# Attention scores moved to the end of TensorE's slot, and masks ahead of the attention's addition on VectorE

## The chip, the cores and the metric

One core of one Trainium2 chip. The metric is the device time of one execution, in microseconds (us), as the median over several runs. Engines are named as in the profile: PE is TensorE (PEld its weight loads), DVE is VectorE, ACT is ScalarE, POOL is GpSimd, SP the engine that issues all DMAs here. A name with q (SPq) is the engine's queue.

## What is computed

x has 8 sequences of 1024 rows with 256 columns. The output is x plus two branches of its layer norm xn: a linear attention with Taylor features (the first part of the kernel, which the change doesn't touch), and a transformer of two layers (the second part). One layer, cut to what matters:

```python
h = shift_token(x)                      # second half of the columns comes from the row before
q, k, v = split(h @ wqkv)               # 8 heads of 64
q, k = rotary_xpos(l2norm(q) * qs, l2norm(k) * ks)
o = softmax(mask(8 * q @ k.T)) @ v      # a row sees itself and the 128 rows before
x = x + o @ wo
h = shift_token(x)
h = (h - mean(h)) / sqrt(var(h) + 1e-5) * lg + lb
a, g = split(h @ w1 + b1)
x = x + (a * gelu(g)) @ w2 + b2
```

## The kernel before

`transformer_block` works on tiles of 128 rows. There are four threads: two streams (four sequences each, one behind another) by two layers. A step is one tile of one thread, 4 x 32 = 128 steps in all; they are numbered n and handed out in turn, so that layer 1 of a stream follows its layer 0. Each step passes through four stages, and all engines run a list of slots in which four neighbouring steps are each at another stage: `cur` (projections, norm and rotation of q and k, their transposes), `att` (scores, softmax, attention, out-projection), `nrm` (residual addition, layer norm), `ffn` (up, GELU, down); `nxt` only has its input transposed. Every engine has its own `slot` function, written out by hand, and takes its instructions strictly in that order; semaphores join the engines, and a wait is on a count that the step's number gives.

PSUM has eight banks, given out by name at L692 to L694. What the change and the steps of the prediction touch:

- TensorE, `slot` from L1446: `scores` of att (L1352 and L1359, 64x64 tiles, first in the slot), `project` K and Q (L1327), `up` (L1431, L1436), `project` V, `prob_T` (L1370, L1374), `down` (L1443), `attend` (L1389 middle, tiles of 128x64; L1399 corners, 64x64), `heads_T` K and Q of cur (L1332), `x_T` of nxt (L1319, L1320), `hn_T` of nrm (L1415), `out_project` of att (L1408). A float32 matmul counts as two instructions, a transpose as one.
- `heads_T` of K waits for `k_unit`, the K normalisation on VectorE (L1069); `scores` waits for `kT_ready` and `qT_ready`, ScalarE's copies (L1235, L1240).
- VectorE, `slot` from L1157: the attention's addition `add_attention` (L1108), `mask_scores` four times (L1079 adds the mask and takes the maximum, L1086), `row_statistics` (L1113 on x1, L1115 on the shifted columns, L1118, L1120), `normalise` (L1093, L1096), `cosines`, `squares`, `gated` (L1142), `rotate`, `layer_norm` (L1125, L1126), `unit_k` (L1069), `add_ffn` (L1149, L1155), `set_mask`, `copy_hnT` (L1132).
- SP, `shift` (L888, L889): waits for `x1_ready`, which L1108 gives, and copies half the columns of x1 one row down into `xsh` by two DMAs. L1115 waits for both. In the same list stand `keep_k`, `place_v` and `keep_v`, copies within SBUF that carry keys and values to the next tile.
- ScalarE, `slot`: `exps` (L1246), copies and squares of k and q, `gelus` (L1268, with a table load), `copy_v`, `copy_pT`, `primed_s` (L1295, an exponential of one column that draws the table load for it there), `copy_oT` (L1259), `copy_kT`, `copy_qT`, `copy_hT`.

The four lines that carry the wait from the addition to the statistics:

```python
sp.wait_ge(x1_ready, n + 1)
sp.dma_start(xsh[s][l][1:113, :], x1[s][l][0:112, P:DIM]).then_inc(shifted[s][l], 16)
...
dve.wait_ge(shifted[s][l], 32 * it + 32)
v.bn_stats(st[:, 1, :], xsh[s][l][:, :]).then_inc(stats, 1)
```

Of the kernel before, what the change touches and what calls it, by code (L numbers as in the profile page):

```python
# [669 lines left out]
def transformer_block(nc, PAIRS, x, xn_d, attn_d, wqkv_s, wo, w1, b1, w2, ln, qk_scale, rotary, masks, ident, out):  # L670
# [6 lines left out]
    with ExitStack() as ctx:  # L677
# [12 lines left out]
        ps = ctx.enter_context(nc.psum_tensor("f_ps", [P, 8, 512], F32))  # L690

        SCORES = (0, 1, 2, 3)  # L692
        XT, HNT, K, V, Q, KT, QT, OT, WO, DOWN = 2, 3, 4, 5, 5, 4, 5, 0, 7, 6
        UP = (6, 7, 4)  # L694

        wo_s = sb("fwo_s", [P, LAYERS, INNER // P, DIM])
# [326 lines left out]
        def _(dve):  # L1023
# [76 lines left out]
            def add_attention(step):  # L1100
                n, s, l, it = step
                xprev = xin[s] if l == 0 else xmid[s]
                if l == 0:
                    dve.wait_ge(xn_in[s], 16 * it + 16)
                if some(it):
                    dve.wait_ge(carried[s][l], 16 * it)
                dve.wait_ge(wo_ps, n + 1)
                v.tensor_tensor(x1[s][l][:, 0:DIM], ps[:, WO, 0:DIM], xprev[:, :], ALU.add).then_inc(x1_ready, 1)  # L1108

            def row_statistics(step):  # L1110
                n, s, l, it = step
                dve.wait_ge(x1_ready, n + 1)
                v.bn_stats(st[:, 0, :], x1[s][l][:, 0:P])  # L1113
                dve.wait_ge(shifted[s][l], 32 * it + 32)
                v.bn_stats(st[:, 1, :], xsh[s][l][:, :]).then_inc(stats, 1)  # L1115
                dve.wait_ge(stats, 2 * n + 1)
                dve.sem_inc(passed_dve, 1)
                v.bn_aggr(mv[:, :], st[:, :, :].rearrange("p a n -> p (a n)")).then_inc(stats, 1)  # L1118
                dve.wait_ge(stats, 2 * n + 2)
                v.tensor_scalar_add(ve[:, :], mv[:, 1:2], LN_EPS).then_inc(var_ready, 1)  # L1120
# [34 lines left out]
                    v.tensor_tensor(yout[s][:, :], ps[:, DOWN, 0:DIM], xb[s][:, :], ALU.add).then_inc(x2_ready, 1)  # L1155

            def slot(nxt, cur, att, nrm, ffn):  # L1157
                if nrm:
                    add_attention(nrm)
                if att:  # L1160
                    for p in range(4):
                        mask_scores(att, p)
                if nrm:
                    row_statistics(nrm)
                if att:
                    normalise(att, 0)
                if cur:
                    cosines(cur, 1, k_ready, k_cosd)
                if att:
                    normalise(att, 1)  # L1170
                if cur:
                    squares(cur, 1, sqk_ready, knorm_ready, ssqk_sum, ssqk_ready)
                if ffn:
                    gated(ffn)
                if cur:
                    rotate(cur, 1, k_cosd, k_turned, k_rotated)
                if nrm:
                    layer_norm(nrm)
                if cur:
                    cosines(cur, 0, q_ready, q_cosd)  # L1180
                if cur:
                    squares(cur, 0, sqq_ready, qnorm_ready, ssqq_sum, ssqq_ready)
                    rotate(cur, 0, q_cosd, q_turned, q_rotated)
                if cur:
                    unit_k(cur)
                if ffn:
                    add_ffn(ffn)
                if nxt:
                    set_mask(nxt)
                if nrm:  # L1190
                    copy_hnT(nrm)
# [4 lines left out]
        def _(act):  # L1196
# [33 lines left out]
            def copy_kT(step):  # L1230
                n, s, l, it = step
                if some(it):
                    act.wait_ge(k_kept[s][l], 16 * it)
                act.wait_ge(kT_ps, n + 1)
                a.activation(kT[s][l][:, :, P:2 * P], ps[:, KT, :].rearrange("p (c n) -> p c n", n=P), ACT.Copy).then_inc(kT_ready, 1)  # L1235

            def copy_qT(step):
                n, s, l, it = step
                act.wait_ge(qT_ps, n + 1)
                a.activation(qT[:, :, :], ps[:, QT, :].rearrange("p (c n) -> p c n", n=P), ACT.Copy).then_inc(qT_ready, 1)  # L1240
# [35 lines left out]
            def slot(nxt, cur, att, nrm, ffn):  # L1276
                if att:
                    for p in range(3):
                        exps(att, p)
                if cur:  # L1280
                    copy_part(cur, 1, K, k_ps, k_ready)
                if att:
                    exps(att, 3)
                if cur:
                    square(cur, 1, k_ready, ssqk_sum, sqk_ready)
                    copy_part(cur, 0, Q, q_ps, q_ready)
                    square(cur, 0, q_ready, ssqq_sum, sqq_ready)
                if ffn:
                    gelus(ffn)
                if cur:  # L1290
                    copy_v(cur)
                if att:
                    copy_pT(att)
                if cur:
                    a.activation(primed_s[:, :], mhalf[:, 0:1], ACT.Exp)  # L1295
                if att:
                    copy_oT(att)
                if cur:
                    copy_kT(cur)
                    copy_qT(cur)  # L1300
                if nxt:
                    copy_hT(nxt)

# [3 lines left out]
        def _(pe):  # L1307
# [22 lines left out]
            def heads_T(step, i, b, done):  # L1330
                for h in range(0, HEADS, 2):
                    last = tr(ps[:, b, h // 2 * P:(h // 2 + 1) * P],  # L1332
                              qk[:, i * HEADS + h:i * HEADS + h + 2, :].rearrange("p h d -> p (h d)"), id_s[:, :])
                last.then_inc(done, 1)

            def scores(step, cur, ffn, p):
                n, s, l, it = step
                if p == 0:
                    pe.wait_ge(kT_ready, n + 1)
                    pe.wait_ge(qT_ready, n + 1)  # L1340
                if p == 2 and cur:
                    pe.wait_ge(hT_ready, cur[0] + 1)
                if p == 2 and ffn:
                    pe.wait_ge(hnT_ready, ffn[0] + 1)
                for k in range(2):
                    middle, corner = k * 256 + k * HALF, k * 256 + (1 - k) * P
                    for q in (p, p + 1):
                        h = PAIRS_OF_HEADS[q][k]
                        r = slice(h % 2 * HD, h % 2 * HD + HD)
                        for half in range(2):  # L1350
                            rows = slice(half * HALF, half * HALF + HALF)
                            mm(ps[rows, SCORES[q], middle:middle + P], qT[r, h // 2, rows], kT[s][l][r, h // 2, HALF:HALF + P],  # L1352
                               start=True, stop=True)
                    for q in (p, p + 1):
                        h = PAIRS_OF_HEADS[q][k]
                        r = slice(h % 2 * HD, h % 2 * HD + HD)
                        for half in range(2):
                            rows = slice(half * HALF, half * HALF + HALF)
                            last = mm(ps[rows, SCORES[q], corner:corner + HALF], qT[r, h // 2, rows],  # L1359
                                      kT[s][l][r, h // 2, half * BAND:half * BAND + HALF], start=True, stop=True)  # L1360
                        if k == 1:
                            last.then_inc(score_ps, 1)
# [81 lines left out]
                last.then_inc(down_ps, 1)  # L1444

            def slot(nxt, cur, att, nrm, ffn):  # L1446
                if att:
                    for p in (0, 2):
                        scores(att, cur, ffn, p)
                if cur:  # L1450
                    project(cur, 1, K, k_ps)
                    project(cur, 0, Q, q_ps)
                if ffn:
                    up(ffn, cur, nrm)
                if cur:
                    pe.wait_ge(q_ready, cur[0] + 1)
                    project(cur, 2, V, v_ps)
                if att:
                    prob_T(att)
                if ffn:  # L1460
                    down(ffn)
                if att:
                    if nrm and not ffn:
                        pe.wait_ge(x1_ready, nrm[0] + 1)
                    attend(att)
                if cur:
                    pe.wait_ge(k_unit, cur[0] + 1)
                    heads_T(cur, 1, KT, kT_ps)
                    pe.wait_ge(v_ready, cur[0] + 1)
                    pe.wait_ge(q_rotated, cur[0] + 1)  # L1470
                    heads_T(cur, 0, QT, qT_ps)
                if nxt:
                    x_T(nxt)
                if nrm:
                    hn_T(nrm)
                if att:
                    out_project(att)
# [101 lines left out]
```

## Time and profile before

| | |
|---|---|
| runs | 3824.41 us median of 3 (3824.31 to 3825.34) |
| the profiled execution | 3827.29 us, span 3825.5 us |
| PE busy | 3661.6 us, 96% of the span |
| DVE busy | 2835.6 us, 74% |
| ACT busy | 2756.8 us, 72% |
| POOL busy | 1247.2 us, 33% |
| mean granted clock of TensorE | 0.985 |

Busy times are of the profiled execution, and so are all rows below. The span is the time from its first to its last instruction; the execution's own time has 1.8 us more around it. A busy TensorE is one with matmuls under way; their ends are modelled, so neighbouring matmuls overlap in a timeline and the distance from start to start is what one takes. The second part begins near 1100 us and has the steady slots from about 1230 to 3781 us.

### The profile page before, as it was taken

How to read it: one execution, taken by the hardware profiler on the slowest of the kernel's cores; microseconds unless marked ns; L12 is line 12 of the kernel's file. 1: busy time of each engine (PE TensorE's matmuls, PEld its weight loads, DVE VectorE, ACT ScalarE, POOL GpSimd, SP SyncE). 2: the span in 40 equal slices, each digit the busy share in tenths (PEclk: the TensorE clock that was granted, in tenths of full speed). 3: DMA queues.
4: the chain of work that ended last, by engine and by line, in shares of the span. 5: the costliest groups of instructions: out<-in, count | busy, mean ns of one | idle time of the engine just before them, and what ended most of it. 6: DMA issues, size and time to landing. Idle time of an engine off the chain costs nothing.

```text
span 3825.5 us, 92479 instructions
## 1 busy us (share of the span) xinstructions
PE 3661.6 (96%) x34784; PEld 2549.4 (67%) x34784; DVE 2835.6 (74%) x8672; ACT 2756.8 (72%) x6076; POOL 1247.2 (33%) x1319
## 2 busy tenths in 40 slices
PE   7999999999958999999999999999999999999997
PEld 3434444443426777777777777777777777777776
DVE  5766776776655877877877877877878778778774
ACT  5687677768735777777777777777777777777774
POOL 2211221221123433333333333333334334333332
PEclk9999999999978999999999999999999999999999
DMA  2100100110031222222222222222222222222210
GB/s 80 35 24 13 35 24 13 34 35 13 13 119 47 54 68 63 57 68 63 57 68 62 57 68 60 59 68 62 57 64 64 60 64 61 63 63 59 66 49 24
DMA packets 213054, 202.04 MB, mean 53 GB/s; under 512 B 31744, under 2 KB 171264, under 8 KB 211968
## 3 DMA queue, kind: packets, MB, share of 16 engines
q1 hardware_dynamic: 212608, 196.12, 18.6%
q8 instruction: 277, 4.54, 0.5%
q14 instruction: 169, 1.38, 0.1%
HBM read 46.87 MB, written 25.17 MB: 19 GB/s over the span
## 4 chain that ended last, share of the span: by engine, by line
PE 44%; DVE 13%; issue 6%; SPq 3%; DMA 2%; POOL 1%; ACT 0%; DVEq 0%; POOLq 0%
PE f_ps L1327 11%; PE f_ps L1431 9%; PE f_ps L1443 5%; PE f_ps L1408 5%; DVE pr L1096 3%; PE f_ps L1332 3%; PE f_ps L1352 2%; PE f_ps L1389 2%; DVE cosine L1046 2%; PE f_ps L1370 2%; DMA xsh<-x 2%; DVE act_u L1142 2%; DVE ssq L1054 2%; PE f_ps L1399 1%; DVE pr L1079 1%
## 5 line engine op out<-in xcount | busy, mean ns | idle before, releaser
L1246 ACT ACTIVATE pr<-pr,nmax,rnorm 128x192 f32<-128x192 f32 x1024 | 545.9, 535 | 347.1 <-DVE nmax L1086 347.1
L1327 PE MATMUL f_ps<-wqkv_s,hT 128*128 128x512 f32 x1536 | 717.5, 603 | 10.9 <-ACT hT L1208 5.5
L488 ACT ACTIVATE weights<-t_ps,four_s 128x1024 f32<-128x1024 f32 (+3 forms) x768 | 630.5, 906 | 103.6 <-PE t_ps L593 98.7
L1431 PEld LDWEIGHTS f_ps<-hnT,w_s 128*128 128x128 f32 x5120 | 593.4, 192 | 60.4 <-issue 58.8
L1431 PE MATMUL f_ps<-hnT,w_s 128*128 128x128 f32 x5120 | 594.8, 276 | 0.8 <-DVE hnT L1132 0.8
L1096 DVE TENSOR_SCALAR pr<-pr,rsum 128x192 f32<-128x192 f32 x1024 | 450.2, 500 | 9.0
L1327 PEld LDWEIGHTS f_ps<-wqkv_s,hT 128*128 128x128 f32 x1536 | 272.5, 190 | 270.1 <-issue 246.0
L973 POOL TENSOR_TENSOR rstd<-ve,f_mhalf 128x1 f32<-128x1 f32 x128 | 81.5, 637 | 1121.6 <-DVE ve L1120 1121.6
L985 POOL TENSOR_TENSOR turned<-qk,rot 128x256 f32<-128x256 f32 x512 | 394.7, 795 | 57.5 <-ACT qk L1213 44.0
L392 DVE SCALAR_TENSOR_TENSOR weights<-weights,causal_s 128x512 f32<-128x512 f32 x256 | 210.9, 826 | 244.8 <-ACT weights L488 244.8
L1079 DVE CUSTOM_DVE_ANT_0 pr<-f_ps,mask 128x192 f32<-128x192 f32 x1024 | 326.3, 355 | 68.3 <-PE f_ps L1359 66.6
L593 PE MATMUL t_ps<-qkT 96*128 96x512 bf16 (+3 forms) x1536 | 345.0, 333 | 14.5 <-ACT weights L488 9.8
L607 PE MATMUL t_ps<-weights,vals 128*32 128x512 f32 (+3 forms) x3072 | 332.6, 506 | 26.7 <-DVE weights L392 20.2
L1443 PE MATMUL f_ps<-w_s,act_u 128*128 128x256 f32 x1536 | 354.3, 380 | 1.6 <-DVE act_u L1142 1.3
L999 POOL TENSOR_TENSOR rnorm<-ssq,f_mhalf 128x8 f32<-128x8 f32 x128 | 248.1, 1938 | 298.8 <-DVE ssq L1056 298.8
L593 PEld LDWEIGHTS t_ps<-qkT 96*128 96x128 bf16 x1536 | 107.5, 98 | 325.3 <-ACT weights L488 244.7
L1443 PEld LDWEIGHTS f_ps<-w_s,act_u 128*128 128x128 f32 x1536 | 281.9, 190 | 37.4 <-DVE act_u L1142 3.0
L270 POOL TENSOR_TENSOR yT<-yT,den 128x1024 f32<-128x1024 f32 x24 | 58.1, 2423 | 681.2 <-DVE den L319 681.2
L992 POOL TENSOR_TENSOR rnorm<-ssq,f_mhalf 128x8 f32<-128x8 f32 x128 | 210.6, 1645 | 198.3 <-DVE ssq L1056 198.3
L1132 DVE TENSOR_SCALAR hnT<-f_ps,ln_s 128x128 f32<-128x128 f32 x256 | 93.3, 405 | 227.8 <-PE f_ps L1415 227.8
L1259 ACT ACTIVATE oT<-f_ps 128x512 f32<-128x512 f32 x128 | 76.5, 598 | 252.1 <-PE f_ps L1399 252.1
L1408 PE MATMUL f_ps<-fwo_s,oT 128*128 128x256 f32 x1024 | 242.7, 380 | 1.9 <-ACT oT L1259 1.8
(132 smaller groups left out, 7070.3 us busy)
## 6 DMA issues: line engine op xcount, KB each, us to landing
vw<-vw SPq DMA_DIRECT2D x628, 128.0 KB, 2.4
kT<-kT SPq DMA_DIRECT2D x124, 256.0 KB, 2.6
xs<-x_dram SPq DMA_DIRECT2D x8, 1024.0 KB, 7.9
xn_dram<-xn SPq DMA_DIRECT2D x8, 1024.0 KB, 5.3
attn_dram<-ao SPq DMA_DIRECT2D x8, 1024.0 KB, 4.5
xin<-xn_dram SPq DMA_DIRECT2D x64, 128.0 KB, 2.2
xres<-x_dram SPq DMA_DIRECT2D x64, 128.0 KB, 2.0
xres<-attn_dram SPq DMA_DIRECT2D x64, 128.0 KB, 2.2
```

Source lines behind the costliest of these rows:

```text
L488: a.activation(weights[:, 2 * (u % UNITS):2 * (u % UNITS) + 2, c:512], ps[:, unit_bank(n):unit_bank(n) + 2, c:512], ACT.Square, bias=four_ ...
L593: last = mm(ps[:, unit_bank(n) + k, c:512], qkT[:, 1, place, j * P:(j + 1) * P], qkT[:, 0, place, half * 512 + c:(half + 1) * 512], start= ...
L607: last = mm(ps[h * VP:(h + 1) * VP, half, c:512], vals[:, j, g * GH + h, :], weights[:, 4 * i % (2 * UNITS) + h, c:512], start=(j == 0), s ...
L985: g.tensor_tensor(turned[:, heads, f], qk[:, heads, z], sines, ALU.mult).then_inc(done, 1)
L999: g.tensor_tensor(rnorm[:, :HEADS], ssq[:, :HEADS], mhalf[:, :HEADS], ALU.pow).then_inc(qnorm_ready, 1)
L1079: last = v.tensor_tensor_reduce(out=chances(h), in0=ps[:, SCORES[p], k * 256:k * 256 + BAND], in1=mask[s][l][:, HALF - k * HALF:HALF - k * ...
L1096: last = v.tensor_scalar_mul(chances(h), chances(h), rsum[:, h:h + 1])
L1246: last = a.activation(chances(h), chances(h), ACT.Exp, bias=nmax[:, h:h + 1], scale=rnorm[:, h:h + 1], accum_out=psum[:, h:h + 1])
L1327: last = mm(ps[:, b, :], rows, wqkv_s[:, l, c, i * INNER:(i + 1) * INNER], start=(c == 0), stop=(c == KC - 1))
L1408: last = mm(ps[:, WO, 0:DIM], oT[:, c, :], wo_s[:, l, c, :], start=(c == 0), stop=(c == INNER // P - 1))
L1431: last = mm(ps[:, UP[j // 2], o:o + P], w1_s[:, l, c, half * FULL + j * P:half * FULL + j * P + P], hnT[:, c, :], start=(c == 0), stop=(c ...
L1443: last = mm(ps[:, DOWN, 0:DIM], act_u[:, j, :], w2_s[:, l, j, :], start=(j == 0), stop=(j == FB - 1))
```

## The change

On TensorE `scores` leaves the head of the slot, where it worked on att. It now works on cur, behind `heads_T` and `attend` of the same slot, and `attend` comes behind `heads_T` instead of ahead of it. The waits in `scores` and ahead of the Q projection are others, since the banks are given out anew. VectorE takes `mask_scores` of att ahead of `add_attention`. ScalarE copies kT and qT ahead of the exponential that draws the table load.

```diff
--- before.py
+++ after.py
@@ -690,7 +690,7 @@
         ps = ctx.enter_context(nc.psum_tensor("f_ps", [P, 8, 512], F32))
 
         SCORES = (0, 1, 2, 3)
-        XT, HNT, K, V, Q, KT, QT, OT, WO, DOWN = 2, 3, 4, 5, 5, 4, 5, 0, 7, 6
+        XT, HNT, K, V, Q, KT, QT, OT, WO, DOWN = 4, 5, 4, 5, 5, 4, 5, 6, 7, 3
         UP = (6, 7, 4)
 
         wo_s = sb("fwo_s", [P, LAYERS, INNER // P, DIM])
@@ -1155,12 +1155,11 @@
                     v.tensor_tensor(yout[s][:, :], ps[:, DOWN, 0:DIM], xb[s][:, :], ALU.add).then_inc(x2_ready, 1)
 
             def slot(nxt, cur, att, nrm, ffn):
-                if nrm:
-                    add_attention(nrm)
                 if att:
                     for p in range(4):
                         mask_scores(att, p)
                 if nrm:
+                    add_attention(nrm)
                     row_statistics(nrm)
                 if att:
                     normalise(att, 0)
@@ -1292,12 +1291,11 @@
                 if att:
                     copy_pT(att)
                 if cur:
+                    copy_kT(cur)
+                    copy_qT(cur)
                     a.activation(primed_s[:, :], mhalf[:, 0:1], ACT.Exp)
                 if att:
                     copy_oT(att)
-                if cur:
-                    copy_kT(cur)
-                    copy_qT(cur)
                 if nxt:
                     copy_hT(nxt)
 
@@ -1333,15 +1331,15 @@
                               qk[:, i * HEADS + h:i * HEADS + h + 2, :].rearrange("p h d -> p (h d)"), id_s[:, :])
                 last.then_inc(done, 1)
 
-            def scores(step, cur, ffn, p):
+            def scores(step, att, ffn, p):
                 n, s, l, it = step
                 if p == 0:
                     pe.wait_ge(kT_ready, n + 1)
                     pe.wait_ge(qT_ready, n + 1)
-                if p == 2 and cur:
-                    pe.wait_ge(hT_ready, cur[0] + 1)
+                if p == 0 and not att and some(n):
+                    pe.wait_ge(pT_ready, 3 * n)
                 if p == 2 and ffn:
-                    pe.wait_ge(hnT_ready, ffn[0] + 1)
+                    pe.wait_ge(x2_ready, ffn[0] + 1)
                 for k in range(2):
                     middle, corner = k * 256 + k * HALF, k * 256 + (1 - k) * P
                     for q in (p, p + 1):
@@ -1444,11 +1442,10 @@
                 last.then_inc(down_ps, 1)
 
             def slot(nxt, cur, att, nrm, ffn):
-                if att:
-                    for p in (0, 2):
-                        scores(att, cur, ffn, p)
                 if cur:
                     project(cur, 1, K, k_ps)
+                    if ffn:
+                        pe.wait_ge(hnT_ready, ffn[0] + 1)
                     project(cur, 0, Q, q_ps)
                 if ffn:
                     up(ffn, cur, nrm)
@@ -1459,16 +1456,19 @@
                     prob_T(att)
                 if ffn:
                     down(ffn)
-                if att:
-                    if nrm and not ffn:
-                        pe.wait_ge(x1_ready, nrm[0] + 1)
-                    attend(att)
                 if cur:
                     pe.wait_ge(k_unit, cur[0] + 1)
                     heads_T(cur, 1, KT, kT_ps)
                     pe.wait_ge(v_ready, cur[0] + 1)
                     pe.wait_ge(q_rotated, cur[0] + 1)
                     heads_T(cur, 0, QT, qT_ps)
+                if att:
+                    if nrm and not ffn:
+                        pe.wait_ge(x1_ready, nrm[0] + 1)
+                    attend(att)
+                if cur:
+                    for p in (0, 2):
+                        scores(cur, att, ffn, p)
                 if nxt:
                     x_T(nxt)
                 if nrm:
```

## Rows read from the trace of the kernel before

**Rows 1.** Busy us (x instructions) of each engine in one stretch, then granted clock, DMA.
```profile
1500.00:2500.00 1000.00, 997.67 (x10335) 786.49 (x10334) 789.91 (x2721) 742.32 (x1847) 383.55 (x387) 1.00 0.24 63
```

**Rows 2.** Groups by line, 1350 to 3700 us: xcount, busy us, mean ns, idle before.
```profile
L1408 PE MATMUL f_ps<-fwo_s,oT 128*128 128x256 f32 x912 | 215.7, 379 | 0.0
```

**Rows 3.** Waits, 1500 to 3500 us: total us, times, longest us.
```profile
DVE hnT L1132 <- PE f_ps L1415: 173.1, 98, 2.3
...
DVE st L1115 <- DMA xsh<-x: 46.3, 49, 2.1
```

**Rows 4.** Timeline of TensorE, one slot: start us, us from start to end, xcount.
```profile
2001.63 3.70 PE L1327 MATMUL f_ps<-wqkv_s,hT 128*128 128x512 f32 x8
2005.17 4.63 PE L1431 MATMUL f_ps<-hnT,w_s 128*128 128x128 f32 x40
...
2013.10 2.76 PE L1443 MATMUL f_ps<-w_s,act_u 128*128 128x256 f32 x12
2015.78 1.09 PE L1389 MATMUL f_ps<-pT,vw 128*64 128x128 f32 x16
...
2017.43 1.09 PE L1332 MATMUL f_ps<-f_id,qk 128*128 128x128 f32 x8
2018.36 0.27 PE L1319 MATMUL f_ps<-f_id,xmid 128*128 128x128 f32 x1
...
2018.58 0.38 PE L1415 MATMUL f_ps<-f_id,hn 128*128 128x128 f32 x2
2018.80 1.89 PE L1408 MATMUL f_ps<-fwo_s,oT 128*128 128x256 f32 x8
2020.62 0.45 PE L1352 MATMUL f_ps<-kT,qT 64*64 64x128 f32 x8
...
2022.12 3.70 PE L1327 MATMUL f_ps<-wqkv_s,hT 128*128 128x512 f32 x8
```

**Rows 5.** Groups by line of ScalarE, 1350 to 3700 us.
```profile
L1295 ACT ACT_TABLE_LOAD x114 | 146.3, 1283 | 2.1
...
L1240 ACT ACTIVATE qT<-f_ps 128x512 f32<-128x512 f32 x114 | 67.5, 592 | 0.0
```

**Rows 6.** Timeline of VectorE in the same slots.
```profile
2005.36 0.29 DVE L1115 BATCH_NORM_STATS2 st<-xsh 128x6 f32<-128x128 f32 x1 [0.58 <-DMA xsh<-x]
...
2006.12 0.17 DVE L1093 RECIPROCAL rsum<-psum 128x4 f32<-128x4 f32 x1
2006.32 2.03 DVE L1096 TENSOR_SCALAR pr<-pr,rsum 128x192 f32<-128x192 f32 x4
...
2009.61 1.26 DVE L1096 TENSOR_SCALAR pr<-pr,rsum 128x192 f32<-128x192 f32 x4
...
2011.58 1.63 DVE L1142 SCALAR_TENSOR_TENSOR act_u<-f_ps,b_s,act_u 128x128 f32<-128x128 f32 x6
...
2016.24 0.69 DVE L1069 TENSOR_TENSOR qk<-qk,rnorm 128x512 f32<-128x512 f32 x1
...
2019.00 0.73 DVE L1132 TENSOR_SCALAR hnT<-f_ps,ln_s 128x128 f32<-128x128 f32 x2 [1.53 <-PE f_ps L1415]
2020.80 0.42 DVE L1108 TENSOR_TENSOR x<-f_ps,xmid 128x256 f32<-128x256 f32 x1 [1.07 <-PE f_ps L1408]
2021.71 0.36 DVE L1079 CUSTOM_DVE_ANT_0 pr<-f_ps,mask 128x192 f32<-128x192 f32 x1 [0.48 <-PE f_ps L1359]
...
2024.98 0.28 DVE L1113 BATCH_NORM_STATS2 st<-x 128x6 f32<-128x128 f32 x1
```

**Rows 7.** Timeline of SP's queue, and landing times of L889's DMAs.
```profile
2002.72 0.59 SPq L888 DMA_DIRECT2D xsh<-x  x1
...
DMA to landing us min/median/max: 2.0/2.0/3.8
```

**Rows 8.** Busy us in two stretches of the first part, columns as in rows 1.
```profile
188.20:191.60 3.40, 2.65 (x16) 1.47 (x14) 1.35 (x3) 2.71 (x6) 0.00 (x0) 1.00 0.00 0
191.60:195.00 3.40, 3.17 (x12) 0.63 (x12) 1.35 (x3) 1.99 (x5) 0.00 (x0) 0.51 0.00 0
```

## The prediction

> **What bounds the kernel now.** I read the stretches first. In the second part, which takes some 2600 of the 3825 us, TensorE is busy 997.67 of 1000 us at a granted clock of 1.00, while VectorE has 789.91 [rows 1]. So TensorE's list sets the pace, and another engine counts only when it delays that list. The groups by line give the pace: the out-projection makes 8 matmuls a slot, and 912 of them in 2350 us are 114 slots of 20.61 us [rows 2]. There are 128 steps; I take 124 slots as full ones (two at either end run alone). The waits say where VectorE has its spare time: for the transposed norm 173.1 us in 98 slots, and for the DMA that shifts x by a row 46.3 us in 49 of them [rows 3]. The first is slack behind TensorE. The second must be watched, since the change moves what it waits for.
>
> TensorE's own row of one slot [rows 4] shows what is to be saved. Between blocks of different tile size the array pays a little. Twelve matmuls of the down-projection take 2.68 us up to the next block, eight of the out-projection 1.82; the difference of four is 0.86, so one is 0.215 and 0.10 remains behind each. Entering a block of smaller tiles costs about 0.05 more. Leaving the scores costs about 0.10 behind them and 0.10 in the projections (3.54 us for eight, which have twice the columns of 0.215 and so take 3.44); leaving the corners 0.10 and 0.06 (the K and Q transposes take 0.93, at 0.11 each 0.87).
>
> **The change on TensorE.** No instruction is added or removed; blocks move. Gone: out-projection to scores (0.15), scores to projection (0.20), down-projection to attention (0.15), corners to transposes (0.16), together 0.66. New: transposes to attention (0.15) and scores to the transposes of x (0.16), together 0.31; corners to scores is one tile size, 64x64, and I price it at nothing (the bound above is 0.15, as between other small blocks). Saved 0.35 us a slot, times 124 is 43 us, if nothing else ends last. The Trainium skill, page "TensorEngine Tiling (Array Packing)", section "Key Properties", says that changing the tiling mode, not just the tile, drains TensorE. By that rule five switches become three, and the time would come out lower; the trace agrees on the price of a switch, and the time by it is the third rival.
>
> **The change in bank numbers and waits.** New banks cost nothing by themselves. The waits for them: scores two and three wait for the FFN addition (bank 3), which VectorE issues right behind the K normalisation, 2 us before; the Q projection waits for the transposed norm, which VectorE copied while the out-projection ran. ScalarE's copies of kT and qT now come ahead of the table load of 1.28 us [rows 5]. The copy of qT takes 0.59 and begins about 1.2 us after the K transposes begin, so both are there after 1.8 us, while scores begin at 2.5: covered by the attention products. If that cover went, scores would start late by what is missing. The table load now lies ahead of the copy of oT: 1.8 + 1.28 + 0.20 + 0.60 is 3.9 us, and the out-projection begins at 4.47. Covered as well. On SP nothing changes place, but the shift's wait for x1 ends later, and behind it stand the loads and the copy of kT, which have slots of slack.
>
> **What is now in a circle.** Two things meet. Scores of the current step now need kT and qT of the same slot, and the transposed norm comes behind the scores, so VectorE, which goes in order, cannot take the masks until it has copied that norm, though the scores are ready before. And VectorE's addition now stands directly ahead of the row statistics, which need x shifted by a DMA that starts only when the addition is done. Before, the masks and maxima (3.27 us) stood between the two and hid most of the transfer. Now nothing does.
>
> I follow one slot, from H, the start of the K transposes [rows 4, 6, 7]:
> - K and Q transposes 0.87 and drain 0.10: attention at 0.97. Attention took 2015.78 to 2017.43, 1.65, less its exit 0.10: scores at 2.52. Scores 1.50 less entry 0.05: x transposes at 3.97. These 0.22 and 0.06: norm transposes at 4.25.
> - VectorE begins to copy the transposed norm 0.42 later (2018.58 to 2019.00), at 4.67, and takes 0.73: 5.40.
> - Masks and maxima 2021.71 to 2024.98, 3.27: 8.67. The addition 0.42: 9.09.
> - The transfer. Where VectorE was seen waiting for it, 2.64 us passed from SP's first issue (2002.72) to the statistics (2005.36). The bounds: landing takes 2.0 at least and in the median, 3.8 at most, behind 0.6 of the first issue [rows 7]. SP's copies of values wait for the attention products, done at 2.6, so its queue should be free at 9.09 and I stay near the low end, 2.75: 11.84.
> - Statistics to the first reciprocal 0.76 (2005.36 to 2006.12): 12.60. From there to the end of the K normalisation 10.81 (2006.12 to 2016.93), in which VectorE waits for nobody: 23.41. To TensorE's next K transposes 0.05, an estimate: 23.46.
>
> That is the new slot, against 20.61: 2.85 us more. TensorE's work is only 20.14 of it. Where does it wait? The second of the six gated products comes at 12.60 + 5.46 + 0.55 = 18.61, the down-projection follows in 2.6 us up to 21.2, and the K transposes wait to 23.46. So it idles about 2.2 us in one piece there and 1 us ahead of the down-projection. VectorE idles from its mask copy to 4.67 and during the transfer.
>
> **The sum.** 124 x 2.85 = 353 us. The profiled execution took 3827.3 us, so 4181; the median of the runs is 2.9 lower, so 4178. The 43 us on TensorE are in this already, since the circle is built from its shorter blocks; they are not taken off again.
>
> **Both ends.** Low: 2.6 for the transfer takes off 19 us. GpSimd's products run beside VectorE's normalisations; if they met less, the first four of these might take 1.26 as the second four did, instead of 2.03 [rows 6], and 0.77 would go per slot, 95 us. Half of that and the transfer give about 4100. High: a transfer of 3.3, halfway to its worst, adds 68 us: 4250; the clock adds more, next.
>
> **Rivals.**
> *The clock falls too.* In the first part the granted clock went from 1.00 to 0.51 behind a stretch of 3.4 us in which TensorE was busy 2.65 and had several short waits [rows 8]; those are the levels 2.4 and 1.2 GHz. The new idle piece of 2.2 us is longer than those waits, and it lies just ahead of the transposes, attention and scores, which are in the circle. At 1.2 GHz for 3.4 us as in that row, 1.7 us of work is lost. If that came in every slot it would be 25.2 us and 4390; in two of three slots 1.13 x 124 = 140, so 4320. Against it: blocks on both sides are dense. The Trainium skill, page "TensorE: Matmul & The Clock Gate", says that the throttled state is the default and activity releases it; by that the clock is lost here where it was never lost in rows 1. Chance 0.25.
>
> *The transfer is hidden anyway.* Were x shifted in time, the slot would be 23.46 - 2.75 + 0.2 = 20.9 us, and the kernel 3824 + 36 = 3860. For it: nothing but that half the slots show no wait now; against it: those slots had 3.27 us of masks in between, which are gone. Chance 0.04.
>
> *Faster: the drains alone count.* Here the circle would not close: the K normalisation is done before the down-projection is, 14.0 us after the projections begin. Then the slot is 20.61 - 0.35 and the time 3781. It decides as soon as VectorE's row from masks to K normalisation, with addition and transfer, fits into about 15 us; it takes 3.27 + 0.42 + 2.75 + 0.76 + 10.81 = 18.0. Chance 0.04.
>
> A remaining 0.01 is for no change, where small savings meet small waits. The forecast itself has 0.66. The bound between them is 0.2%, about 8 us, what a measurement of this kernel can tell from no change. The forecast, the clock and the hidden transfer (3860) lie above it, together 0.95. Faster 0.04, same 0.01, slower 0.95. The range goes from 4090, the low end of the forecast, to 4360, which takes in the clock in up to seven of eight slots; left out are the hidden transfer, the faster case, and the worst of clock and transfer together.
>
> **What would show it.** In the changed profile: slots of 23 to 24 us by the count of out-projections; VectorE waiting for the DMA of the shift in every slot, some 2.3 us each, instead of 46.3 us in half of them; TensorE waiting at the K transposes for the K normalisation, about 2.2 us, and at the down-projection for the gated products; no drain between corners and scores; TensorE's busy share near 86%. If the wait for the shift were under 1 us a slot, or the clock stood at 0.9 or less over the stretch, the step above that fails is named by that row.

## The result, and the profile after

The changed kernel takes 4245.1 us (median of 6 runs, 4242.7 to 4295.9) against 3824.4 us before: a ratio of 1.112, 95% interval 1.107 to 1.117. That is 421 us more, where 354 were forecast (4178), and inside the range of 4090 to 4360.

The first lines of the page, and the clock by slices, of the changed kernel:

```profile
PE 3783.3 (89%) x34784; PEld 2603.1 (61%) x34784; DVE 2834.9 (67%) x8672; ACT 2760.3 (65%) x6076; POOL 1268.9 (30%) x1319
...
PEclk9999999999799999999999999999999999999998
```

TensorE's busy share fell from 96% to 89%, with the same 34784 matmuls. It waits more, and the same work also keeps it busy longer, 3783.3 us instead of 3661.6, in part through the slower clock of some stretches, which is shown further on. The same stretch as in [rows 1], with the same columns:

```profile
1500.00:2500.00 1000.00, 899.64 (x8890) 696.00 (x8890) 681.21 (x2345) 641.51 (x1591) 337.19 (x335) 0.98 0.20 54
```

TensorE is busy 899.64 us of 1000 instead of 997.67, VectorE 681.21 instead of 789.91, and the granted clock is 0.98 instead of 1.00. No engine is full any more, as is to be expected if they wait for one another in a circle. The out-projections of 1350 to 3700 us, which answer to [rows 2]:

```profile
L1406 PE MATMUL f_ps<-fwo_s,oT 128*128 128x256 f32 x784 | 185.5, 380 | 0.0
```

784 matmuls are 98 slots in 2350 us instead of 114: 24.0 us each instead of 20.6. And the waits of 1500 to 3500 us, which answer to [rows 3] (who waited for whom, total us, times, longest us):

```profile
DVE hnT L1132 <- PE f_ps L1413: 394.1, 84, 5.8
...
DVE st L1115 <- DMA xsh<-x: 198.3, 83, 4.2
PEld f_ps L1330 <- DVE qk L1069: 189.2, 84, 2.3
...
PE f_ps L1330 <- DVE qk L1069: 155.5, 84, 1.9
...
PEld f_ps L1441 <- DVE act_u L1142: 56.4, 84, 0.7
```

VectorE now waits for the shift in each of its 83 slots, 2.4 us a time; before it was 49 of 98, 0.9 us a time. TensorE waits at the K transposes for the K normalisation in every slot (its weight loads 189.2 us, its matmuls 155.5, the same time seen on two rows), and a little at the down-projection for the gated products.

TensorE's timeline of one slot, to be read against [rows 4]:

```profile
2006.64 1.09 PE L1330 MATMUL f_ps<-f_id,qk 128*128 128x128 f32 x8 [1.89 <-DVE qk L1069]
2007.67 1.09 PE L1387 MATMUL f_ps<-pT,vw 128*64 128x128 f32 x16
2008.69 0.70 PE L1397 MATMUL f_ps<-pT,vw 64*64 64x64 f32 x32
2009.21 0.40 PE L1350 MATMUL f_ps<-kT,qT 64*64 64x128 f32 x8
...
2010.66 0.33 PE L1317 MATMUL f_ps<-f_id,xmid 128*128 128x128 f32 x1
...
2011.15 1.89 PE L1406 MATMUL f_ps<-fwo_s,oT 128*128 128x256 f32 x8
2012.88 3.60 PE L1325 MATMUL f_ps<-wqkv_s,hT 128*128 128x512 f32 x8
...
2025.17 2.86 PE L1441 MATMUL f_ps<-w_s,act_u 128*128 128x256 f32 x12 [0.43 <-DVE act_u L1142]
2029.92 1.09 PE L1330 MATMUL f_ps<-f_id,qk 128*128 128x128 f32 x8 [1.89 <-DVE qk L1069]
```

The corners (L1397) take 0.52 us to the first score instead of 0.62 to the K transposes, and the scores take 1.45 us up to the next block instead of 1.50: no pause shows between two blocks of 64x64 tiles. The slot, from one set of K transposes to the next, is 2029.92 - 2006.64 = 23.28 us. VectorE in the same slot, against [rows 6]:

```profile
2011.35 0.73 DVE L1132 TENSOR_SCALAR hnT<-f_ps,ln_s 128x128 f32<-128x128 f32 x2 [4.23 <-PE f_ps L1413]
...
2015.28 0.42 DVE L1108 TENSOR_TENSOR x<-f_ps,xmid 128x256 f32<-128x256 f32 x1
...
2018.30 0.29 DVE L1115 BATCH_NORM_STATS2 st<-xsh 128x6 f32<-128x128 f32 x1 [2.27 <-DMA xsh<-x]
...
2019.06 0.17 DVE L1093 RECIPROCAL rsum<-psum 128x4 f32<-128x4 f32 x1
...
2029.17 0.69 DVE L1069 TENSOR_TENSOR qk<-qk,rnorm 128x512 f32<-128x512 f32 x1
```

### The profile page after: what moved, and what is told of

It is laid out like the page before. It is cut to its first block, busy times and chain, and to the rows that moved or that the text cites. A ratio compares the mean times of both kernels' runs of the same rounds, so it can differ in the third digit from the quotient of the medians.

```text
span 4243.4 us, 92480 instructions
## 1 busy us (share of the span) xinstructions
PE 3783.3 (89%) x34784; PEld 2603.1 (61%) x34784; DVE 2834.9 (67%) x8672; ACT 2760.3 (65%) x6076; POOL 1268.9 (30%) x1319
## 4 chain that ended last, share of the span: by engine, by line
DVE 38%; PE 16%; issue 11%; DMA 7%; SPq 2%; POOL 0%; ACT 0%; DVEq 0%; POOLq 0%; ACTq 0%
DVE pr L1096 8%; DVE pr L1079 7%; DMA xsh<-x 6%; DVE cosine L1046 5%; DVE act_u L1142 4%; PE f_ps L1387 4%; DVE ssq L1054 4%; PE f_ps L1330 3%; PE f_ps L1350 3%; PE f_ps L1397 2%; DVE qk L1069 2%; DVE qk L1063 2%; SPq L888 2%; PE f_ps L1357 1%; DVE x L1108 1%
## 5 line engine op out<-in xcount | busy, mean ns | idle before, releaser
L1325 PE MATMUL f_ps<-wqkv_s,hT 128*128 128x512 f32 x1536 | 703.7, 594 | 9.4 <-ACT hT L1207 5.4
L1234 ACT ACTIVATE kT<-f_ps 128x512 f32<-128x512 f32 x128 | 76.4, 597 | 667.7 <-PE f_ps L1330 667.7
L1325 PEld LDWEIGHTS f_ps<-wqkv_s,hT 128*128 128x128 f32 x1536 | 282.6, 191 | 266.4 <-issue 245.6
L985 POOL TENSOR_TENSOR turned<-qk,rot 128x256 f32<-128x256 f32 x512 | 416.9, 844 | 24.1 <-DMA w_s<-w_dram 12.8
L1096 DVE TENSOR_SCALAR pr<-pr,rsum 128x192 f32<-128x192 f32 x1024 | 414.6, 465 | 9.0
L1441 PE MATMUL f_ps<-w_s,act_u 128*128 128x256 f32 x1536 | 371.8, 393 | 53.4 <-DVE act_u L1142 53.4
L1330 PE MATMUL f_ps<-f_id,qk 128*128 128x128 f32 x1024 | 145.3, 287 | 247.6 <-DVE qk L1069 247.6
L1330 PEld LDWEIGHTS f_ps<-f_id,qk 128*128 128x128 f32 x1024 | 113.4, 144 | 300.6 <-DVE qk L1069 300.6
```

The costliest lines, as they stand in the source:

```text
L985: g.tensor_tensor(turned[:, heads, f], qk[:, heads, z], sines, ALU.mult).then_inc(done, 1)
L1096: last = v.tensor_scalar_mul(chances(h), chances(h), rsum[:, h:h + 1])
L1325: last = mm(ps[:, b, :], rows, wqkv_s[:, l, c, i * INNER:(i + 1) * INNER], start=(c == 0), stop=(c == KC - 1))
L1330: last = tr(ps[:, b, h // 2 * P:(h // 2 + 1) * P], qk[:, i * HEADS + h:i * HEADS + h + 2, :].rearrange("p h d -> p (h d)"), id_s[:, :])
L1441: last = mm(ps[:, DOWN, 0:DIM], act_u[:, j, :], w2_s[:, l, j, :], start=(j == 0), stop=(j == FB - 1))
```

## The experiments

Edits are given against the kernel that each expectation names. In the text, "slot" without more is the undisturbed one, from end to end of the K normalisation: most slots have that length, and the mean is longer by those in which the clock falls or a transfer of the shift lands late. The theory: TensorE and VectorE wait for one another once a slot, in a circle that holds the transfer of the shift, and the clock adds to it. The rivals: one half of the change is the whole loss; or the long slots have nothing to do with the clock.

### VectorE's half taken back

```diff
+                if nrm:
+                    add_attention(nrm)
                 if att:
                     for p in range(4):
                         mask_scores(att, p)
                 if nrm:
-                    add_attention(nrm)
                     row_statistics(nrm)
```

> The changed kernel with VectorE's addition put back ahead of the masks; TensorE's new order stays. Theory (a circle of TensorE and VectorE with the transfer of the shift exposed in it): the addition must now wait for the out-projection, about 6.5 us after the K transposes begin, but the 2.6 us of transfer pass behind 3.3 us of masks. 6.5 + 0.4 + 3.3 + 0.2 + 0.76 + 10.80 + 0.05 is 22.0 us a slot, 1.4 more than before, so 3995 us (3960 to 4040), no wait of VectorE for the shift, granted clock 1.00 in the steady stretch. Rival 1 (the transfer is the whole loss, TensorE's order is free): 20.3 us a slot, 3780. Rival 2 (TensorE's order is the whole loss): 4200 or more.

Measured: 4009.8 us, ratio to before 1.048 (1.047 to 1.050), within the range expected. Its waits, 1500 to 3500 us:

```profile
DVE hnT L1132 <- PE f_ps L1414: 384.7, 91, 4.2
...
PEld f_ps L1331 <- DVE qk L1069: 180.5, 91, 2.3
...
DVE x L1108 <- PE f_ps L1407: 98.9, 91, 1.4
...
DVE st L1115 <- DMA xsh<-x: 2.2, 5, 0.7
```

The wait for the shift is gone, 2.2 us in all, and 235 of the 421 us with it. But the kernel is still 184 us slower than before, with TensorE's weight loads waiting 2.0 us a slot at the K transposes instead of 2.25, and VectorE waiting 1.1 us a slot for the out-projection before it can add. So TensorE's half costs by itself: slots are 21.9 us, as the walk around the circle gave (22.0). Both rivals fall.

### VectorE's half alone

```diff
-                if nrm:
-                    add_attention(nrm)
                 if att:
                     for p in range(4):
                         mask_scores(att, p)
                 if nrm:
+                    add_attention(nrm)
                     row_statistics(nrm)
```

> The kernel before with VectorE's half of the change alone: masks ahead of the addition, TensorE's order, banks and ScalarE's order as before. Theory: masks begin 0.4 us before the projections, then 3.7 for masks and addition, 2.6 for the transfer, 0.76 and 10.80: the K normalisation ends 17.4 us after the projections begin, where TensorE wants it at 15.8. Slot 22.1 to 22.2 us, 4020 (3980 to 4060), the wait for the shift 2.3 us in every slot. Rival (VectorE's order only costs together with TensorE's): 3824.

Measured: 4061.0 us, ratio 1.062 (1.060 to 1.063), 1 us above the range expected.

```profile
DVE st L1115 <- DMA xsh<-x: 214.7, 89, 4.2
...
PEld f_ps L1369 <- DVE pr L1096: 82.5, 184, 1.9
PEld f_ps L1442 <- DVE act_u L1142: 59.8, 89, 0.7
```

The slot is 22.2 us as expected, the wait for the shift 2.4 us in every one of 89. TensorE waits at the probabilities' transposes (L1369) and the down-projection (L1442), because everything behind the statistics is late. The mean slot is 22.4 us, which accounts for most of the 41 us over the middle of the expectation: an uncovered transfer that lands late (the longest wait is 4.2 us) makes its slot longer. The halves alone cost 236 and 184 us, together 420, against 421 for the whole. That fit is partly luck: in undisturbed slots it is 1.7 + 1.4 = 3.1 us against 2.8 for the two together, and the whole change has the clock's loss on top, as the next run but one shows.

### The transfer half covered

```diff
                 if nrm:
                     add_attention(nrm)
-                    row_statistics(nrm)
                 if att:
                     normalise(att, 0)
+                if nrm:
+                    row_statistics(nrm)
```

> The changed kernel with the row statistics moved behind the first reciprocal and its four normalisations, so that these cover the transfer; the masks stay ahead of the addition. Theory: the wait of 2.4 us a slot goes, 23.28 - 2.38 is 20.9 us a slot, and since GpSimd's products now begin after the first four normalisations these may take 1.26 instead of 2.03, which brings the circle to TensorE's own 20.2. So 3780 to 3870, and the wait for the shift under 0.5 us a slot. Rival (what the transfer hid is paid elsewhere, a late root of the variance holds up the rotation): above 3950.

Measured: 4026.4 us, ratio 1.053 (1.051 to 1.054): better by 219 us, yet far from the 3780 to 3870 expected, and above 3950, where a rival was put. The rival's mechanism was not it, though: no row of the waits has VectorE behind GpSimd. VectorE's timeline, and two rows of GpSimd's:

```profile
2004.76 1.01 DVE L1096 TENSOR_SCALAR pr<-pr,rsum 128x192 f32<-128x192 f32 x4
...
2007.24 0.29 DVE L1115 BATCH_NORM_STATS2 st<-xsh 128x6 f32<-128x128 f32 x1 [1.27 <-DMA xsh<-x]
...
2008.87 2.50 DVE L1096 TENSOR_SCALAR pr<-pr,rsum 128x192 f32<-128x192 f32 x4
...
2008.16 1.06 POOL L973 TENSOR_TENSOR rstd<-ve,f_mhalf 128x1 f32<-128x1 f32 x1 [11.74 <-DVE ve L1120]
2009.13 2.83 POOL L985 TENSOR_TENSOR turned<-qk,rot 128x256 f32<-128x256 f32 x4
```

The four normalisations take 1.01 us, at a time when GpSimd is idle, and so with the reciprocal and L1113 they cover only half of the 2.6 us: VectorE still waits 1.27 us at L1115. I had counted the quicker normalisations as a gain on top of a full cover; they were the cover. And GpSimd's products (L985), which start behind the variance, now fall on the next four, which take 2.50 where they took 1.26 in the kernel before [rows 6]. The transfer needs more work in front of it, which is the experiment "The transfer covered in full".

### TensorE kept busy ahead of the K transposes

```diff
                 if ffn:
                     down(ffn)
+                    for _ in range(2):
+                        mm(ps[:, KT, :], id_s[:, :], wqkv_s[:, 0, 0, 0:INNER], start=True, stop=True)
```

> The changed kernel with two more 128x128x512 matmuls behind the down-projection, into a bank that is free there, their result is not used: 1.7 us of work in the 1.9 us in which TensorE would idle ahead of the K transposes. Theory (the clock falls in some slots behind that idle piece and stretches transposes, attention and scores, which are in the circle): granted clock 1.00 in the steady stretch, every slot 23.3, so about 4170 us (4155 to 4190), faster than the changed kernel's 4245 with more work. Rival (the long slots come from slow landings of the shift, or from something else on VectorE): 4245 or more, long slots as before.

Measured: 4196.2 us, ratio 1.097 (1.095 to 1.098): 49 us faster than the changed kernel, with 1.7 us more work on TensorE in each slot, and 6 us above the range expected. To see why, three stretches of one long slot of the changed kernel, columns as in [rows 1] (the clock is the number ahead of the last two):

```profile
1551.00:1552.80 1.80, 1.03 (x9) 0.86 (x9) 1.26 (x4) 0.27 (x1) 1.80 (x2) 1.00 0.00 0
1552.80:1556.20 3.40, 3.40 (x65) 3.07 (x68) 0.00 (x0) 2.59 (x5) 1.22 (x2) 0.50 0.29 78
1556.20:1560.00 3.80, 3.80 (x74) 3.29 (x66) 1.92 (x10) 1.31 (x4) 0.00 (x0) 1.00 0.64 159
```

and TensorE's timeline there:

```profile
1551.77 1.09 PE L1330 MATMUL f_ps<-f_id,qk 128*128 128x128 f32 x8 [1.89 <-DVE qk L1069]
1552.80 1.98 PE L1387 MATMUL f_ps<-pT,vw 128*64 128x128 f32 x16
1554.70 1.14 PE L1397 MATMUL f_ps<-pT,vw 64*64 64x64 f32 x32
1555.61 0.65 PE L1350 MATMUL f_ps<-kT,qT 64*64 64x128 f32 x8
...
1557.35 0.33 PE L1317 MATMUL f_ps<-f_id,xin 128*128 128x128 f32 x1
```

TensorE had idled 1.89 us before L1330. The clock then stood at 0.50, that is 1.2 instead of 2.4 GHz, and the way from attention to the transposes of x took 4.55 us (1552.80 to 1557.35) instead of 2.99 (2007.67 to 2010.66). That piece is in the circle, and the slot took 24.9 us instead of 23.3. In the trace's record the clock falls 37 times in 116 slots of the steady stretch, and 2 times with the two matmuls added:

```profile
1500.00:2500.00 1000.00, 971.97 (x9266) 725.53 (x9263) 698.93 (x2404) 657.27 (x1632) 344.73 (x343) 1.00 0.21 55
```

The granted clock is 1.00 again. Of the 67 us by which the forecast was short, the clock is 49; where the other 18 come from is told in the part on the sum. The Trainium skill, page "TensorE: Matmul & The Clock Gate", section "Part 1: The HAM clock gate", says that the throttled state is the default and that activity releases it. The trace agrees: with work in the idle piece the clock falls 2 times instead of 37.

How much idle time it takes is not shown. TensorE's matmuls wait for the K normalisation 1.85 us a slot in the changed kernel (155.5 us in 84 slots). In three other experiments they wait nearly as long, 1.58 us with VectorE's half taken back, 1.63 with the transfer half covered and 1.77 with the masks ahead, yet there the clock falls only 3, 3 and 15 times in 116 or 117 slots. Of these four kernels, the changed one alone idles in every slot ahead of the down-projection too, by 0.43 us.

### Masks ahead of the copy of the transposed norm

```diff
                 if att:
-                    for p in range(4):
+                    for p in range(2):
                         mask_scores(att, p)
+                if ffn:
+                    copy_hnT(ffn)
+                if att:
+                    for p in range(2, 4):
+                        mask_scores(att, p)
...
-                if nrm:
-                    copy_hnT(nrm)
```

> The changed kernel with VectorE taking the first two masks ahead of the copy of the transposed norm (which goes between the second and the third), all else as changed: statistics right behind the addition. It opens the other half of the circle alone. Theory: the first scores are there about 3.4 us after the K transposes begin, so 3.4 + 3.3 + 0.7 + 0.5 + 2.6 of transfer + 0.76 + 10.80 + 0.05 is 22.1 us a slot against 23.3, about 4015 us (3990 to 4060). Rival (the transfer is all that matters and the place of the copy nothing): 4245.

Measured: 4046.5 us, ratio 1.058 (1.056 to 1.059). VectorE's place in the list is the other half of the circle: 199 us come back with no instruction fewer. The slot is 22.1 us as expected; the time is 31 us over the expected middle and within its range, with a mean slot of 22.4 and a clock that falls 15 times. The wait moved with it:

```profile
DVE pr L1079 <- PE f_ps L1360: 296.0, 90, 4.7
...
DVE st L1115 <- DMA xsh<-x: 208.6, 89, 3.8
```

VectorE waits at the masks for the scores, and no longer for the norm; the 2.3 us a slot for the shift stay.

### The transfer covered in full

```diff
                 if nrm:
                     add_attention(nrm)
-                    row_statistics(nrm)
                 if att:
                     normalise(att, 0)
...
                 if att:
                     normalise(att, 1)
+                if nrm:
+                    row_statistics(nrm)
```

> The changed kernel with one edit: row statistics behind all eight normalisations, masks behind the copy of the transposed norm as changed. Theory: 9.1 to the end of the addition, 3.6 of normalisations and cosines, 0.96, 6.1, 0.05 is 19.85 us, just under TensorE's 20.15, so 3785 us (3770 to 3830), with little reserve for a slow landing. Rival (GpSimd, whose first work of a slot waits for the variance, now holds up the rotation of K and Q): 3850 or more, with VectorE waiting for the rotation's products.

Measured: 3818.3 us, ratio 0.9986 (0.9978 to 0.9995). One edit takes back all of the 421 us and 6 more. It is 33 us off the 3785 expected, within its bounds: the slot is 20.36 us, and TensorE still waits for VectorE:

```profile
PEld f_ps L1331 <- DVE qk L1069: 47.7, 98, 1.6
...
DVE st L1115 <- DMA xsh<-x: 5.7, 7, 1.1
```

VectorE's timeline, with one row of GpSimd's, shows what the walk (19.85) missed:

```profile
2026.97 1.01 DVE L1096 TENSOR_SCALAR pr<-pr,rsum 128x192 f32<-128x192 f32 x4
...
2029.09 1.01 DVE L1096 TENSOR_SCALAR pr<-pr,rsum 128x192 f32<-128x192 f32 x4
...
2030.97 0.69 DVE L1054 TENSOR_REDUCE ssq<-sq 128x8 f32<-128x512 f32 x1
2031.69 0.70 DVE L1056 TENSOR_SCALAR ssq<-ssq 128x8 f32<-128x8 f32 x1
2032.54 1.75 DVE L1142 SCALAR_TENSOR_TENSOR act_u<-f_ps,b_s,act_u 128x128 f32<-128x128 f32 x6 [0.15 <-ACT act_u L1268]
...
2037.41 0.69 DVE L1069 TENSOR_TENSOR qk<-qk,rnorm 128x512 f32<-128x512 f32 x1
...
2031.64 2.78 POOL L985 TENSOR_TENSOR turned<-qk,rot 128x256 f32<-128x256 f32 x4
```

The normalisations are quick (1.01 twice). But GpSimd's products (L985) now fall on the work behind, where L1056 takes 0.70 us instead of 0.17, and the way from L1054 to the end of the K normalisation takes 7.13 us where the walk put 6.1; the part ahead of it, from the end of the addition, takes 4.13 (2026.84 to 2030.97) where 4.56 were put. So the circle is 20.36, a little over TensorE's own 20.14.

### Both halves of the circle opened

The edits of the two experiments ahead, together.

> As the one before, and the row statistics moved behind all eight normalisations, which take over 3 us and so cover the 2.6 us of transfer. Both halves of the circle are open: 3.4 + 3.3 + 0.7 + 0.5, then about 3.6 of normalisations and cosines, 0.96 of statistics, 6.1 and 0.05 is 18.6 us, less than TensorE's own blocks. Theory: TensorE sets the pace again, with two drains fewer than before: 20.15 to 20.3 us a slot, 3780 us (3765 to 3800), faster than the kernel before. Rival (the drains saved come back as waits of TensorE, or the drains were never on its path): 3824 or more.

Measured: 3781.5 us, ratio 0.989 (0.988 to 0.990): the fastest of all, 43 us under the kernel before, and 1 us from the 3780 expected. Its out-projections of 1350 to 3700 us, its TensorE in 1500 to 3500 us, and its longest wait for the K normalisation:

```profile
L1410 PE MATMUL f_ps<-fwo_s,oT 128*128 128x256 f32 x936 | 221.5, 379 | 0.1
```

```profile
1500.00:3500.00 2000.00, 2000.00 (x21068) 1612.43 (x21061) 1512.79 (x5573) 1529.22 (x3783) 764.25 (x791) 1.00 0.24 64
```

```profile
DVE st L1115 <- DMA xsh<-x: 2.6, 5, 0.8
...
PEld f_ps L1334 <- DVE qk L1069: 0.6, 2, 0.3
```

936 matmuls are 117 slots in 2350 us. TensorE is busy 2000 of 2000 us at full clock and waits 0.6 us in all for the normalisation. Its slot is 20.14 us against 20.49 of [rows 4]: the 0.35 us of the prediction's drains, to the hundredth.

### The same cover in the kernel before

```diff
-                if nrm:
-                    row_statistics(nrm)
                 if att:
                     normalise(att, 0)
...
                 if att:
                     normalise(att, 1)
+                if nrm:
+                    row_statistics(nrm)
```

> The kernel before with the row statistics behind all eight normalisations. A control for the two runs ahead: whether a gain over the kernel before comes from TensorE's order or from the covered transfer. Theory: TensorE has no slack to give there, slots stay 20.5, and only the few stretched by a slow landing shrink (mean 20.6 to 20.5): 3815 us (3805 to 3828). Rival: 3785, as with TensorE's new order.

Measured: 3816.9 us, ratio 0.998 (0.997 to 0.999), close to the 3815 expected. The slot is 20.49 us in the median and in the mean now, instead of 20.49 in the median and 20.57 in the mean. So the cover alone is worth 7 of the 43 us of the run ahead; the other 36 go with TensorE's new order, whose saved switches show once nothing else ends later.

## Why the prediction was right

**Bound and pace.** Right: TensorE set the pace before, 20.6 us a slot, and no longer does. The signs named for the profile came, with the waits for the shift (2.4 us in every slot) and for the K normalisation (1.9 us) near their forecasts. TensorE's busy share was off: 90% over the stretch where 86% was put.

**The drains.** Right, and shown in two ways: no gap between corners and scores in the changed kernel, and a slot shorter by 0.35 us where nothing else ends last. That corners to scores costs nothing was a choice there; the 0.52 us bear it out. So the third rival describes a kernel that exists, but needs two more edits.

**Banks, ScalarE's copies.** Priced at nothing, and nothing was seen: no row of the waits has TensorE behind kT, qT or oT, and the opened kernel, which has them all, loses nothing.

**The walk around the circle.** Each stop from the start of the K transposes (2006.64), predicted and measured in us: copy of the norm 4.67 and 4.71; end of the addition 9.09 and 9.06; statistics 11.84 and 11.66; first reciprocal 12.60 and 12.42; end of the K normalisation 23.41 and 23.22; next K transposes 23.46 and 23.28. The only stop that was off is the transfer, taken at 2.75 where 2.60 passed (2015.28 + 0.42 to 2018.30).

**The sum.** 4178 was 67 us short. The term that was mis-sized is the clock: the forecast had none, and kept it as a rival with a loss in two of three slots (4320). It is one in three, 1.6 us each (24.87 against 23.28; 1.7 was the estimate), 49 us in all. The case between the two held: 4245 lies about midway between the forecast and the rival. The mechanism was the rival's, beside the forecast's circle. The sign named for it, a granted clock of 0.9 or less over the stretch, misses it: with 37 falls the mean is still 0.98.

The other 18 us are seen where the clock hardly falls, with the two matmuls added. There the mean slot is 23.46 us, to the hundredth the forecast's, and yet the kernel takes 4196. That agreement is luck: the circle itself is 0.16 us shorter than forecast (23.30), and late landings, which an uncovered transfer passes on, together with two falls of the clock put as much back, while the forecast took the transfer near its median and late ones only as a bound. The adding up is what was short. The forecast took 124 slots at 2.85 us over 20.61, 353 us. But there are 127 slots from the first to the last of the 128 K normalisations, the mean slot before is 20.57, and that stretch is 368 us longer in this trace than in the one of before. The last few us lie outside it.

**What was only half seen.** The prediction names both halves of the circle, but its rival of the hidden transfer leaves the rest of the slot as it is, 20.9 us. The experiments show that the rest moves with the way in which the transfer is covered: the slot is 20.4 us with the statistics behind all normalisations, and 21.9 with the addition first, which must then wait for the out-projection.

## What to carry to other kernels

Before a step is moved, look at who waits for what it hands on, and what passes in between: the masks had no use for the addition, yet they stood between it and a consumer that has to wait 2.6 us for a DMA, and they were the cover. When a bound engine's block is moved behind another engine's result of the same slot, walk once around, back to the block, with durations from start to start; if that comes out longer than the engine's own work, the move needs an edit in the other engine's list too. And idle time of TensorE can cost a second time, when the clock falls behind it and the slow stretch lies on the path.

## What was not expected of the hardware

Four normalisations of 128x192 take 1.01 us with GpSimd idle, 2.0 beside its products in the kernel before [rows 6], and up to 2.50. An L1056 of 128x8 goes from 0.17 to 0.70 us in the same way. Where VectorE's work lies against GpSimd's was worth about 1 us a slot in two experiments: 1.2 on the second four normalisations in one, 1.0 on the way from L1054 to the K normalisation in the other, part of which is other waits. The Trainium skill, page "SBUF — State Buffer", section "SBUF: two separate sides", says that VectorE and GpSimd share a pair of ports under an exclusive lock: of two instructions that need it, the one that starts first holds it to its end and the other is blocked. The rows agree in direction; that the ports are the cause, and which engine held which, no run here shows.

One of the six runs of the changed kernel took 4295.9 us at a mean granted clock of 0.844, the others 4242.7 to 4247.1 at 0.967 to 0.969. There is no trace of it, so why its clock was lower stays open.
